# Edge stage of a graph layer on one core: VectorE's comparison moved, attribute product in bf16 parts, six waits dropped

## Chip, cores and metric

One Trainium2 chip, one of its cores. The time of a run is the device time of the whole program on that core, in microseconds (us). Engines: TensorE (PE; its weight loads are shown apart as PEld), VectorE (DVE), ScalarE (ACT), GpSimd (POOL) and SyncE (SP), which only issues transfers here. Lower is better.

## What is computed

One layer of a graph network over 50,000 nodes (x is 50000x128, float32) and 50,000 edges (src, dst, 16 attributes each), then a normalization. Edges come sorted by dst. The reference, cut to what matters:

```
edge_input = concat([x[row], x[col], edge_attr], axis=-1)   # row = src, col = dst
h = silu(edge_input @ eW1 + eb1)
m_ij = silu(h @ eW2 + eb2)
agg = segment_sum(m_ij, row, num_segments=50000)
update = silu(concat([x, agg]) @ nW1 + nb1) @ nW2 + nb2
out = layernorm(x + (x + update))
```

## The kernel before

The edges are cut into 98 groups (GROUP = 512 edges, four tiles of 128). Everything is written by hand, one instruction stream per engine, with semaphores between them; a wait on an engine holds all that stands behind it on that engine.

**Plan.** From the indices VectorE and TensorE work out for each edge a row of a table in HBM, in which edges of one source bucket sit together. Meanwhile ScalarE's queue fills that table with zeros and GpSimd gathers the x rows of the first 28 groups' sources.

**Edge loop**, group g on each engine:

- TensorE: the first layer's product for group g in three terms into p_h, attributes (L719), sources (L721), destinations (L723); then turn_dst(g+1) (L677, destinations by a one-hot `pick`), half of a self product for a node block (self_mm, L700), turn_src(g+1) (transposes, L664), q_mm(g-1) (L708, the message times w_agg), look_up(g+1) (L688), the other self half, and the second layer (L733).
- ScalarE: hT (L809), copy_xd (L792), two copies of the self product (L803), mT (L815).
- VectorE: copy_xs(g+1) out of PSUM (L1001), copy_q(g-1) out of PSUM (L1044, L1046), find_pos(g+1) (L1032 to L1038), compare_edges(g+2) (L1011 to L1023), which makes `pick`, `is_coarseT` and each edge's place in its tile.
- GpSimd: four indirect stores of group g's q rows into the table (L556), each followed by none or more indirect gathers of x rows for a group far ahead (L508). Its store of group g waits for copy_q(g).
- SyncE: loads edge rows, windows of x, attributes and node blocks, two to four groups ahead, and stores the self products.

The attributes lie in HBM transposed, 16 rows by all edges; SyncE loads 16x512 float32 a group (load_attr) into one of three buffers, after the product that used the buffer.

**Node stage.** After the last store SyncE reads the table block by block, and all engines sum per node, apply the two node layers and normalize. The change does not touch it.

Waits are given ahead of an instruction: one can ride on the instruction, each further one is an instruction of its own on the engine's queue.

Of the kernel before, what the change touches and what calls it, by code (L numbers as in the profile page):

```python
# [59 lines left out]
def gnn_kernel(nc, E, x, x_wide, xT, src_all, src_idx, dst_idx, dst_g, attrT, w1s, w1d, w1a, eb1, w2, eb2, nw1a, nb1, nw1b, nw2, nb2,  # L60
               out):
    N = x.shape[0]
    DE = attrT.shape[0]
# [23 lines left out]
    u0_dram = nc.dram_tensor("u0_dram", (STORED, P, BLOCK), F32, kind="Internal").ap()  # L87
    q_dram = nc.dram_tensor("q_dram", (P, D), F32, kind="Internal").ap()

    with ExitStack() as ctx:  # L90
# [15 lines left out]
        w_attr = sb("w_attr", [DE, D])  # L106
# [25 lines left out]
        attr = [sb(f"attr{s}", [DE, GROUP]) for s in range(ATTR)]  # L132
# [8 lines left out]
        with ExitStack() as plan:  # L141
# [21 lines left out]
            worst, worst_all, fits = tmp("worst", [P, 1]), tmp("worst_all", [1, 1]), tmp("fits", [1, 1])  # L163
            b_high, b_mid = tmp("b_high", [P, D], BF16), tmp("b_mid", [P, D], BF16)
# [58 lines left out]
        s_scattered = [sem(f"s_scattered{s}") for s in range(Q)]  # L223
        s_src_turned, s_dst_turned, s_pick, s_xsT, s_xdT = (
# [150 lines left out]
        def _(sp):  # L375
# [3 lines left out]
            for dst_sb, src_dram in ((w_src, w1s), (w_dst, w1d), (w_attr, w1a), (w_e2, w2), (w_agg, nw1b), (w_self, nw1a),  # L379
                                     (w_out, nw2)):  # L380
                sp.dma_start(dst_sb[:], src_dram).then_inc(s_weights, 16)
            for dst_sb, src_dram in ((b_e1, eb1), (b_e2, eb2), (b_n1, nb1)):
                sp.dma_start(dst_sb[:], src_dram.rearrange("(p a) -> p a", a=1)).then_inc(s_weights, 16)
# [15 lines left out]
            for g in range(ATTR):  # L399
                load_attr(g)  # L400
# [7 lines left out]
            sp.wait_ge(s_first_row, 16)  # L408
            sp.wait_ge(s_fits_i, 1)
# [41 lines left out]
            with sp.If_eq(sp.to_reg(fit), 1):  # L451
                load_windows(0)
                for g in range(-3, GROUPS):
                    load_edges(edges_dram[min(g + 3, GROUPS - 1)], g + 3)
                    load_windows(g + WINDOWS)
                    if g >= 0:
                        load_attr(g + 3)
                    serve_self(g)
            with sp.Else():
                pass_on_gathered(0)  # L460
                for g in range(-3, GROUPS):
# [3 lines left out]
                    if g >= 0:  # L465
                        load_attr(g + 3)

# [172 lines left out]
        def _(pe):  # L640
# [16 lines left out]
            def turn_src(g):  # L657
# [4 lines left out]
                wait(pe, s_xsT, g)  # L662
# [4 lines left out]
            def turn_dst(g):  # L667
# [5 lines left out]
                wait(pe, s_xdT, g)  # L673
# [37 lines left out]

            pe.wait_ge(s_before_tile, 1)
# [431 lines left out]
```

## Time and profile before

| | us |
|---|---|
| median of 3 runs | 1565.13 (1563.51 to 1565.4) |
| the profiled execution, its own time | 1560.06 |
| its span, first to last instruction | 1558.5 |
| PE busy | 1214.8 (78%) |
| POOL busy | 1046.3 (67%) |
| DVE busy | 753.9 (48%) |
| ACT busy | 464.9 (30%) |

TensorE's mean granted clock was 0.889 of full over the span. A busy time is the union of the recorded durations; of matmuls only the start is recorded, and the end is modelled. "remote" as the releaser of a wait means that the semaphore changed at a moment at which no instruction that updates it is recorded to end.

### The profile page before, as it was taken

To read this page: it belongs to the slowest core of one execution; us is meant where nothing else is said; L and a number is where in the kernel's file an instruction comes from. 1 tells how busy PE (TensorE), PEld (TensorE's weight loads), DVE (VectorE), ACT (ScalarE), POOL (GpSimd) and SP (SyncE) were. 2 spreads that over 40 slices of the span, in tenths; PEclk is the share of its full clock that TensorE was granted. 3 is DMA by queue.
4 is the path that set the end of the run, shared out by engine and by line. 5 is a ranking of instruction groups with operands and counts; after the bars stand their busy time and mean duration, and the time that the engine had idled before them with its cause. 6 is when DMAs were issued, how large, how long until landed. Compare 5 with 4: busy or idle time off the path is not lost.

```text
span 1558.5 us, 21182 instructions
## 1 busy us (share of the span) xinstructions
PE 1214.8 (78%) x6237; PEld 822.9 (53%) x6237; DVE 753.9 (48%) x2820; ACT 464.9 (30%) x846; POOL 1046.3 (67%) x1268
## 2 busy tenths in 40 slices
PE   3813677888898888979888877777777979999895
PEld 3812344454454444645554444444444579888884
DVE  8941244443344343433433433333333458888885
ACT  0000111222232222222222222222222247777774
POOL 8877565665666556656555666666666548899986
PEclk9996698898899888989888887988888979999998
DMA  9997334455565555655655554555454169999994
GB/s 339 413 411 257 94 106 117 140 166 164 158 200 174 160 165 162 191 171 163 185 164 167 158 154 150 164 164 155 155 153 135 53 228 411 410 410 410 407 407 168
DMA packets 183322, 333.48 MB, mean 214 GB/s; under 512 B 25648, under 2 KB 89696, under 8 KB 183205
## 3 DMA queue, kind: packets, MB, share of 16 engines
q1 hardware_dynamic: 136580, 211.68, 40.7%
q0 software_dynamic: 25024, 52.10, 11.3%
q10 hardware_dynamic: 21600, 68.32, 11.1%
q8 instruction: 52, 0.85, 0.2%
q14 instruction: 66, 0.53, 0.1%
HBM read 215.94 MB, written 116.06 MB: 213 GB/s over the span
## 4 chain that ended last, share of the span: by engine, by line
PE 45%; another core or an unknown queue 26%; DMA 8%; issue 7%; ACTq 7%; DVE 3%; ACT 2%; POOL 2%; POOLq 0%; SPq 0%; DVEq 0%
DMA ring<-table 8%; ACTq L782 7%; PE psum L677 6%; PE psum L751 6%; PE psum L721 6%; PE psum L719 5%; PE psum L700 5%; PE psum L733 5%; PE psum L723 5%; PE psum L708 3%; PE psum L766 3%; POOL table L556 1%; PE psum L664 1%; DVE work L1066 1%
## 5 line engine op out<-in xcount | busy, mean ns | idle before, releaser
L556 POOL DMA_INDIRECT table<-qs,pos x391 | 383.1, 980 | 334.8 <-DVE qs L1046 226.5
L508 POOL DMA_INDIRECT ring<-x_d,idx_src x391 | 408.2, 1044 | 119.1 <-issue 119.1
L1001 DVE COPY work<-psum 128x512 f32<-128x512 f32 x98 | 67.8, 692 | 554.4 <-remote 292.2
L677 PEld LDWEIGHTS psum<-work,windows 128*128 128x128 f32 x980 | 176.4, 200 | 147.5 <-issue 130.3
L677 PE MATMUL psum<-work,windows 128*128 128x256 f32 (+1 forms) x980 | 197.2, 350 | 59.0 <-issue 40.0
L700 PE MATMUL psum<-xT_in,w_self 128*128 128x320 f32 x314 | 129.5, 497 | 136.0 <-ACT u_out L803 101.0
L751 PE MATMUL psum<-work,ring 128*128 128x80 f32 x1250 | 157.3, 280 | 28.1 <-DVE work L1066 24.0
L751 PEld LDWEIGHTS psum<-work,ring 128*128 128x128 f32 x1250 | 148.9, 195 | 37.9 <-issue 21.1
L809 ACT ACTIVATE work<-psum,b_e 128x512 f32<-128x512 f32 x98 | 67.4, 687 | 322.0 <-PE psum L723 164.8
L721 PE MATMUL psum<-work,w_src 128*128 128x512 f32 x196 | 133.1, 766 | 36.7 <-DVE work L1001 20.8
L733 PE MATMUL psum<-work,w_e 128*128 128x512 f32 x196 | 122.1, 710 | 21.2 <-ACT work L809 21.2
L719 PE MATMUL psum<-attr,w_attr 16*128 16x512 f32 x196 | 128.3, 738 | 0.0
L700 PEld LDWEIGHTS psum<-xT_in,w_self 128*128 128x128 f32 x314 | 51.6, 207 | 141.6 <-issue 141.6
L1046 DVE COPY qs<-psum 128x512 f32<-128x512 f32 x98 | 67.5, 689 | 108.5 <-remote 88.8
L723 PE MATMUL psum<-work,w_dst 128*128 128x512 f32 x196 | 119.4, 696 | 0.0
L803 ACT COPY u_out<-psum 128x320 f32<-128x320 f32 x129 | 54.9, 425 | 202.9 <-remote 131.5
L1018 DVE SCALAR_TENSOR_TENSOR same<-edge_rows,bucket,earlier 128x128 f16<-128x128 f16 x392 | 114.0, 343 | 0.0
L792 ACT COPY work<-psum 128x512 f32<-128x512 f32 x98 | 57.4, 586 | 176.1 <-issue 86.0
L708 PE MATMUL psum<-w_agg,work 128*128 128x128 f32 x784 | 105.2, 277 | 3.5 <-ACT work L815 3.5
L815 ACT ACTIVATE work<-psum,b_e 128x512 f32<-128x512 f32 x98 | 67.5, 689 | 132.2 <-remote 74.7
L1011 DVE TENSOR_SCALAR work<-edge_rows,row_f 128x512 f32<-128x512 f16 x196 | 96.9, 536 | 19.4 <-DMA edge_rows<-edges_dram 19.2
L766 PE MATMUL psum<-w_out,work 128*128 128x128 f32 (+1 forms) x782 | 105.4, 282 | 0.0
(123 smaller groups left out, 1624.4 us busy)
## 6 DMA issues: line engine op xcount, KB each, us to landing
ring<-table SPq DMA_DIRECT2D x79, 528.0 KB, 11.1
table<-empty ACTq DMA_DIRECT2D x9, 4224.0 KB
edge_rows<-edges_dram SPq DMA_DIRECT2D x98, 384.0 KB
windows<-x_wide_d SPq DMA_DIRECT2D x98, 320.0 KB
xT_in<-xT_d SPq DMA_DIRECT2D x78, 320.0 KB
out<-windows ACTq DMA_DIRECT2D x78, 320.0 KB, 6.2
u_dram<-u_out SPq DMA_DIRECT2D x64, 320.0 KB
own_x<-x_d SPq DMA_DIRECT2D x48, 320.0 KB, 8.2
```

The lines of the kernel that those rows point to most:

```text
L508: pool.indirect_dma_start(rows, None, x[:, :], bass.IndirectOffsetOnAxis(ap=idx[:, g * TILES + t:g * TILES + t + 1], axis=0)).then_inc(don ...
L556: pool.indirect_dma_start(table[:, :], bass.IndirectOffsetOnAxis(ap=pos[:, g * TILES + t:g * TILES + t + 1], axis=0), q[g % Q][:, t, :], None,
L677: last = nc.tensor.matmul(p_dst[:, tiles], window[g % WINDOWS][:, j, :], pick[g % 2][:, places], start=j == 1, stop=j == 4, skip_group_che ...
L700: nc.tensor.matmul(p_self[:, 0:cols.stop - cols.start], w_self[:], xT_in[i % SELF][:, cols], start=True, stop=True).then_inc(s_self_mm, 1)
L708: last = nc.tensor.matmul(p_q[g % 2][:, t * D:(t + 1) * D], mT[g % 2][:, t * P:(t + 1) * P], w_agg[:], start=True, stop=True)
L719: nc.tensor.matmul(p_h, w_attr[:], attr[g % ATTR][:], start=True, stop=False)
L721: nc.tensor.matmul(p_h, w_src[:], xsT[g % 2], start=False, stop=False)
L723: nc.tensor.matmul(p_h, w_dst[:], xdT[g % 2], start=False, stop=True).then_inc(s_h_mm, 1)
L733: nc.tensor.matmul(p_m, w_e2[:], hT[g % 2], start=True, stop=True).then_inc(s_m_mm, 1)
L751: last = nc.tensor.matmul(u_bucket(b, k), slots_in[b % SLOTS_IN][:, k, 0:D], owner[b % 3][:, k, :].rearrange("s (r p) -> s r p", r=NODE_ROWS),
L766: last = nc.tensor.matmul(psum[2 + b % 2][0:p, j * D:(j + 1) * D], uT[b % 2][:, j * p:(j + 1) * p], w_out[:], start=False, stop=True, skip ...
L1018: last = V.scalar_tensor_tensor(out=same[:, t, :], in0=buckets[:, t * P:(t + 1) * P], scalar=bucket[:, c:c + 1], in1=earlier[:], op0=ALU.i ...
```

## The change

Three edits.

1. VectorE's loop: compare_edges(g+2) stands right behind copy_xs(g+1), ahead of copy_q(g-1) and find_pos(g+1).
2. The attribute term: each float32 is split into three bf16 parts. The host lays the attributes out by batches of 8 groups (128 rows by 512). For each batch VectorE makes the three parts (split_attr, four instructions), SyncE stores them twice to an HBM scratch (store_attr), and load_attr reads a 96-row bf16 tile a group from it: the three parts, twice. Two bf16 products, one of 96 rows (attributes' parts against the high and the middle part of the weights) and one of 48 rows (against the low part), replace the float32 product of 16 rows. The weights' parts are made once, by eight VectorE instructions (s_w_attr).
3. Six waits a group that other waits imply are left out: four on TensorE (s_xsT before turn_src, s_xdT before turn_dst, s_hT before the attribute product, s_mT before the second layer) and two on VectorE (s_dst_turned and s_look_mm in compare_edges).

The diff, without declarations and the host's reshaping:

```diff
             def load_attr(g):
                 if g >= GROUPS:
                     return
+                k, r = divmod(g, BATCH)
+                wait(sp, s_attr_out, 32 * (k + 1))
                 wait(sp, s_h_mm, g - ATTR + 1)
-                sp.dma_start(attr[g % ATTR][:], attrT[:, g * GROUP:(g + 1) * GROUP]).then_inc(s_attr[g % ATTR], 16)
+                rows = attr_dram[k, :, :, r * DE:(r + 1) * DE, :].rearrange("j i f e -> (j i) f e")
+                sp.dma_start(attr[g % ATTR][:], rows).then_inc(s_attr[g % ATTR], 16)
+
+            def store_attr(k):
+                sp.wait_ge(s_attr_split, 4 * (k + 1))
+                for j in range(2):
+                    sp.dma_start(attr_dram[k, j].rearrange("i p e -> p i e"), attr_parts[:]).then_inc(s_attr_out, 16)
+
+            def serve_attr(g):
+                k = g // BATCH + 1
+                if g < 0 or k >= BATCHES:
+                    return
+                if g % BATCH == 0:
+                    sp.wait_ge(s_attr_split, 4 * k)
+                    sp.dma_start(attr_left[:], attr_batches[k]).then_inc(s_attr_in, 16)
+                if g % BATCH == 4:
+                    store_attr(k)
...
-            for g in range(ATTR):
-                load_attr(g)
...
             sp.wait_ge(s_first_row, 16)
+            store_attr(0)
+            for g in range(ATTR):
+                load_attr(g)
             sp.wait_ge(s_fits_i, 1)
...
                     if g >= 0:
                         load_attr(g + 3)
+                    serve_attr(g)
                     serve_self(g)
...
                 wait(pe, s_gathered[pair(g)], pair_gathered(g))
-                wait(pe, s_xsT, g)
...
                 wait(pe, s_pick, g + 1)
-                wait(pe, s_xdT, g)
...
                 wait(pe, s_attr[g % ATTR], 16 * (g // ATTR + 1))
-                wait(pe, s_hT, g)
-                nc.tensor.matmul(p_h, w_attr[:], attr[g % ATTR][:], start=True, stop=False)
+                nc.tensor.matmul(p_h, w_attr_hm[:], attr[g % ATTR][:], start=True, stop=False)
+                nc.tensor.matmul(p_h, w_attr_l[0:PARTS, :], attr[g % ATTR][0:PARTS, :], start=False, stop=False)
...
                 wait(pe, s_hT, g + 1)
-                wait(pe, s_mT, g)
...
+            def split_attr(k):
+
+                wait(dve, s_attr_in, 16 * (k + 1))
+                wait(dve, s_attr_out, 32 * k)
+                V.tensor_copy(attr_parts[:, 0, :], attr_left[:]).then_inc(s_attr_split, 1)
+                dve.wait_ge(s_attr_split, 4 * k + 1)
+                V.tensor_tensor(attr_left[:], attr_left[:], attr_parts[:, 0, :], ALU.subtract).then_inc(s_attr_split, 1)
+                dve.wait_ge(s_attr_split, 4 * k + 2)
+                V.tensor_copy(attr_parts[:, 1, :], attr_left[:]).then_inc(s_attr_split, 1)
+                dve.wait_ge(s_attr_split, 4 * k + 3)
+                V.tensor_tensor(attr_parts[:, 2, :], attr_left[:], attr_parts[:, 1, :], ALU.subtract).then_inc(s_attr_split, 1)
...
                 wait(dve, s_edges[g % ROWS_IN], 16 * (g // ROWS_IN + 1))
-                wait(dve, s_dst_turned, g - 1)
...
                 last.then_inc(s_pick, 1)
-                wait(dve, s_look_mm, g - 1)
...
                 copy_xs(g + 1)
+                compare_edges(g + 2)
                 if g > 0:
                     copy_q(g - 1)
                 find_pos(g + 1)
-                compare_edges(g + 2)
+                if g % BATCH == 1 and g // BATCH + 1 < BATCHES:
+                    split_attr(g // BATCH + 1)
```

VectorE in the middle of the edge loop before, from copy_xs of one group to copy_xs of the next (work<-psum is xsT, qs is q):

```order
L1001 COPY work<-psum 128x512
L1044 COPY qs<-local 128x4
L1046 COPY qs<-psum 128x4x128
L1032 TENSOR_TENSOR hit<-psum,is_fine 128x20
L1035 TENSOR_REDUCE look<-hit 128x4
L1038 SCALAR_TENSOR_TENSOR pos<-look,base_row 128x4
L1011 TENSOR_SCALAR work<-edge_rows,row_f 128x4x128 x2
L1015 TENSOR_SCALAR is_coarseT<-edge_rows,row_f 128x512
L1018 SCALAR_TENSOR_TENSOR same,in_tile<-edge_rows,bucket,earlier 128x128 x4
L1023 SCALAR_TENSOR_TENSOR base_row<-in_tile,base_row 128x4
```

And the same stretch of the changed program (line numbers are those of the changed file):

```order
L1055 COPY work<-psum 128x512
L1064 TENSOR_SCALAR work<-edge_rows,row_f 128x4x128 x2
L1067 TENSOR_SCALAR is_coarseT<-edge_rows,row_f 128x512
L1070 SCALAR_TENSOR_TENSOR same,in_tile<-edge_rows,bucket,earlier 128x128 x4
L1075 SCALAR_TENSOR_TENSOR base_row<-in_tile,base_row 128x4
L1096 COPY qs<-local 128x4
L1098 COPY qs<-psum 128x4x128
L1084 TENSOR_TENSOR hit<-psum,is_fine 128x20
L1087 TENSOR_REDUCE look<-hit 128x4
L1090 SCALAR_TENSOR_TENSOR pos<-look,base_row 128x4
```

The copy of q and find_pos moved behind the eight instructions of the comparison. TensorE in the middle of the edge loop before, one group, with the semaphores that each row waits for:

```order
L719 MATMUL psum<-attr,w_attr 128x512 [waits s_hT,s_attr2]
L721 MATMUL psum<-work,w_src 128x512 [waits s_xsT]
L723 MATMUL psum<-work,w_dst 128x512 [waits s_xdT]
L677 MATMUL psum<-work,windows 128x256 [waits s_xdT,s_pick,s_window2]
...
L664 MATMUL psum<-ident,ring 128x128 [waits s_xsT,s_gathered2]
...
L708 MATMUL psum<-w_agg,work 128x128 [waits s_q,s_mT]
...
L733 MATMUL psum<-work,w_e 128x512 [waits s_mT,s_hT]
```

And of the changed program:

```order
L748 MATMUL psum<-attr,w_attr_hm 128x512 [waits s_attr0]
L749 MATMUL psum<-attr,w_attr_l 128x512
L751 MATMUL psum<-work,w_src 128x512 [waits s_xsT]
L753 MATMUL psum<-work,w_dst 128x512 [waits s_xdT]
L706 MATMUL psum<-work,windows 128x256 [waits s_pick,s_window2]
...
L694 MATMUL psum<-ident,ring 128x128 [waits s_gathered4]
...
L737 MATMUL psum<-w_agg,work 128x128 [waits s_q,s_mT]
...
L762 MATMUL psum<-work,w_e 128x512 [waits s_hT]
```

One attribute product became two, and four waits are gone. SyncE ahead of the loop in the changed program, where before the three attribute loads stood ahead of the store of first_dram:

```order
L433 DMA first_row<-first_dram 1x98 [waits s_plan_out]
L409 DMA attr_dram<-attr_parts 128x3x512 [waits s_attr_split,s_first_row]
L409 DMA attr_dram<-attr_parts 128x3x512
L404 DMA attr<-attr_dram 96x1x512 [waits s_attr_out] x3
L439 TENSOR_LOAD fits_i [waits s_fits_i]
```

The stores of batch 0 and the wait for them to land now stand between the plan and the first window's load.

## Rows read from the trace of the kernel before

**Rows 1.** Windows by stage: stretch, its length, then busy time of each engine, clock, DMA share, GB/s.

```profile
0.00:107.20 107.20, 51.80 (x413) 47.95 (x413) 89.66 (x128) 0.00 (x0) 86.74 (x78) 1.00 1.01 386
...
176.50:1208.00 1031.50, 836.95 (x3413) 491.35 (x3413) 399.28 (x1656) 239.20 (x432) 636.10 (x645) 0.88 0.53 159
...
1249.00:1558.50 309.50, 268.12 (x2189) 249.31 (x2189) 241.30 (x940) 209.33 (x391) 252.32 (x473) 0.95 0.92 358
```

**Rows 2.** Waits: who waited for whom, us in total, times, longest.

```profile
DVE work L1001 <- remote: 292.2, 32, 22.6
POOL table L556 <- DVE qs L1046: 226.5, 75, 5.2
```

**Rows 3.** Timeline, POOL (start, us, what): last early gather, first issues of runs, one last issue.

```profile
167.71 0.94 POOL L508 DMA_INDIRECT ring<-x_d,idx_src  x1 [0.30 <-issue]
...
700.52 0.97 POOL L556 DMA_INDIRECT table<-qs,pos  x1 [3.84 <-DVE qs L1046]
...
713.62 1.00 POOL L556 DMA_INDIRECT table<-qs,pos  x1 [4.39 <-DVE qs L1046]
...
724.53 0.98 POOL L556 DMA_INDIRECT table<-qs,pos  x1 [2.22 <-DVE qs L1046]
...
740.31 0.98 POOL L508 DMA_INDIRECT ring<-x_d,idx_src  x1 [0.30 <-issue]
...
745.26 1.00 POOL L556 DMA_INDIRECT table<-qs,pos  x1 [3.97 <-DVE qs L1046]
```

**Rows 4.** Timeline, PE: attribute and source products of three groups.

```profile
702.88 2.07 PE L719 MATMUL psum<-attr,w_attr 16*128 16x512 f32 x2
...
713.66 1.12 PE L719 MATMUL psum<-attr,w_attr 16*128 16x512 f32 x2
714.71 1.12 PE L721 MATMUL psum<-work,w_src 128*128 128x512 f32 x2
...
721.83 1.12 PE L719 MATMUL psum<-attr,w_attr 16*128 16x512 f32 x2
```

**Rows 5.** Timeline of all engines, 728 to 748, rows chosen.

```profile
728.62 1.06 PE L708 MATMUL psum<-w_agg,work 128*128 128x128 f32 x8
...
731.61 0.69 DVE L1046 COPY qs<-psum 128x512 f32<-128x512 f32 x1 [2.02 <-remote]
...
733.04 0.18 DVE L1032 TENSOR_TENSOR hit<-psum,is_fine 128x20 f32<-128x20 f32 x1 [0.73 <-remote]
733.22 1.02 PE L723 MATMUL psum<-work,w_dst 128*128 128x512 f32 x2
...
735.87 0.69 ACT L815 ACTIVATE work<-psum,b_e 128x512 f32<-128x512 f32 x1 [1.71 <-remote]
...
736.88 0.60 PE L664 MATMUL psum<-ident,ring 128*128 128x128 f32 x4
...
740.18 0.69 ACT L809 ACTIVATE work<-psum,b_e 128x512 f32<-128x512 f32 x1 [3.62 <-remote]
...
743.15 0.69 DVE L1001 COPY work<-psum 128x512 f32<-128x512 f32 x1 [7.16 <-remote]
...
747.15 2.07 PE L719 MATMUL psum<-attr,w_attr 16*128 16x512 f32 x2
```

**Rows 6.** Groups by line and form: the bf16 products of 512 columns in the node stage.

```profile
L762 PE MATMUL psum<-b_parts,ones_bf 128*128 128x512 bf16 x78 | 29.8, 382 | 0.0
```

**Rows 7.** Timeline, DVE: first and last instruction of one compare_edges.

```profile
700.65 1.06 DVE L1011 TENSOR_SCALAR work<-edge_rows,row_f 128x512 f32<-128x512 f16 x2
...
703.09 0.23 DVE L1023 SCALAR_TENSOR_TENSOR base_row<-in_tile,base_row 128x4 f32<-128x4 f32 x1
```

**Rows 8.** Groups by line, DVE: the nearest rows to split_attr's instructions.

```profile
L902 DVE TENSOR_TENSOR dst_rel<-dst_i,tile_i 98x512 f32<-98x512 int32 x1 | 0.6, 644 | 0.0
...
L912 DVE CAST edges_b<-coarse 98x512 f16<-98x512 f32 x1 | 0.4, 422 | 0.0
```

**Rows 9.** Timeline, DVE: the first compare_edges of the loop.

```profile
102.36 0.88 DVE L1011 TENSOR_SCALAR work<-edge_rows,row_f 128x512 f32<-128x512 f16 x2 [10.09 <-DMA edge_rows<-edges_dram]
```

More of the change, by code:

```diff
@@ L87, in gnn_kernel @@
     u0_dram = nc.dram_tensor("u0_dram", (STORED, P, BLOCK), F32, kind="Internal").ap()
+    attr_dram = nc.dram_tensor("attr_dram", (BATCHES, 2, 3, P, GROUP), BF16, kind="Internal").ap()
     q_dram = nc.dram_tensor("q_dram", (P, D), F32, kind="Internal").ap()
@@ L131, in gnn_kernel @@
         xsT, xdT, hT, mT = ([work[:, (4 + 2 * k + s) * GROUP:(5 + 2 * k + s) * GROUP] for s in range(2)] for k in range(4))
-        attr = [sb(f"attr{s}", [DE, GROUP]) for s in range(ATTR)]
+        attr = [sb(f"attr{s}", [TWICE, GROUP], BF16) for s in range(ATTR)]
+        attr_left, attr_parts = sb("attr_left", [P, GROUP]), sb("attr_parts", [P, 3, GROUP], BF16)
         is_coarseT = [sb(f"is_coarseT{s}", [P, GROUP], F16) for s in range(2)]
@@ L223, in gnn_kernel @@
         s_scattered = [sem(f"s_scattered{s}") for s in range(Q)]
+        s_attr_in, s_attr_split, s_attr_out, s_w_attr = (sem(n) for n in ("s_attr_in", "s_attr_split", "s_attr_out", "s_w_attr"))
         s_src_turned, s_dst_turned, s_pick, s_xsT, s_xdT = (
@@ L466, in _ @@
                         load_attr(g + 3)
+                    serve_attr(g)
             sp.wait_ge(s_src_turned, GROUPS)
@@ L710, in q_mm @@
                 last.then_inc(s_q_mm, 1)
+            pe.wait_ge(s_w_attr, 8)
             pe.wait_ge(s_before_tile, 1)
@@ L991, in _ @@
                                    ).then_inc(s_b_parts, 1)
+            V.tensor_copy(w_high[:], w_attr[:]).then_inc(s_w_attr, 1)
+            V.tensor_scalar(is_first[:], row_f[0:TWICE, 0:1], PARTS - 0.5, None, ALU.is_lt).then_inc(s_w_attr, 1)
+            V.tensor_scalar(is_second[:], row_f[0:TWICE, 0:1], PARTS - 0.5, None, ALU.is_gt).then_inc(s_w_attr, 1)
+            dve.wait_ge(s_w_attr, 3)
+            V.tensor_tensor(w_attr[:], w_attr[:], w_high[:], ALU.subtract).then_inc(s_w_attr, 1)
+            V.tensor_scalar(w_sum[:], w_high[:], is_first[:, 0:1], None, ALU.mult).then_inc(s_w_attr, 1)
+            dve.wait_ge(s_w_attr, 5)
+            V.tensor_copy(w_mid[:], w_attr[:]).then_inc(s_w_attr, 1)
+            dve.wait_ge(s_w_attr, 6)
+            V.tensor_tensor(w_attr_l[:], w_attr[:], w_mid[:], ALU.subtract).then_inc(s_w_attr, 1)
+            V.scalar_tensor_tensor(out=w_attr_hm[:], in0=w_mid[:], scalar=is_second[:, 0:1], in1=w_sum[:], op0=ALU.mult,
+                                   op1=ALU.add).then_inc(s_w_attr, 1)
             dve.wait_ge(s_ids, 1)
@@ L1118, in by_block, with by_batch @@
         return rows
+    def by_batch(attr):
+        batch, de = P // attr.shape[1], attr.shape[1]
+        groups = -(-padded_edges(E) // (GROUP * batch)) * batch
+        rows = np.zeros((groups * GROUP, de), attr.dtype)
+        rows[:E] = attr
+        return rows.reshape(groups // batch, batch, GROUP, de).transpose(0, 1, 3, 2).reshape(groups // batch, P, GROUP)
     no_node = ((-(-N // BLOCK) * BLOCK) + BUCKET * np.arange(pads)).astype(src.dtype)
```

18 lines of the change are left out of this document (13 added, 5 removed).

## The prediction

> **What bounds the kernel now.** I read the windows by stage first [rows 1]. The edge loop proper, groups 2 to 93, fills 176.5 to 1208: 1031.5 us for 92 groups, 11.2 us each. TensorE is busy in 837 of them and GpSimd in 636, so no engine is full. The node stage (309.5 us) and the table fill ahead of the loop (DMA share 1.01 until 107.2) don't contain an edited line that matters, so the question is what an average group of 11.2 us waits for.
>
> A group in which TensorE waits for nothing takes 8.17 us: from the start of one attribute product to the next, 713.66 to 721.83, at full clock [rows 4]. The missing 3 us a group come in lumps. GpSimd's issues tell the rhythm: it restarts after a pause at 700.52, 713.62, 724.53 and 745.26 [rows 3]. Between the first and the last lie 44.7 us and 27 issues of 1.28 us (0.98 and 0.30 between them), that is four groups' q: 34.6 us of issues and 10.1 us of pauses. Each pause ends with copy_q, and over the run GpSimd waited for it 75 times, 226.5 us [rows 2].
>
> Next, what makes q late. In the last third of that cycle TensorE's records run ahead of what the other engines see [rows 5]. The products of q end at 729.68 by the record (728.62 + 1.06), and VectorE is let go at 731.61; the first layer ends at 734.24, and ScalarE starts hT at 740.18, 5.9 us later; the transposes end at 737.48, and VectorE copies xs at 743.15, 5.7 us later. All three consumers had been idle. So TensorE's signals arrive late. They do so only inside long GpSimd runs: this run began at 724.53 and its last issue ended at 741.29 [rows 3], and by 743.15 everything was released at once. Signals in the first microseconds of a run, or while GpSimd rests, are on time; q's at 731.61, 7.1 us into this run, is the first late one. VectorE's wait for xs with releaser "remote", 292.2 us in 32 waits [rows 2], is this. During the late stretch signals are spaced: q's at 731.61 and the look-up's at 733.04, 1.43 us apart, though the look-up is four products of five columns each and has two waits. That reads as 0.71 us for each wait that TensorE passes in such a stretch. Between mT's release at 735.87 and hT's at 740.18 lie four waits and three products, 4.3 us, which does not contradict it (2.97 us of products by the record, or six such steps).
>
> When TensorE then idles for its own chain through ScalarE it comes back at half clock (1.2 GHz instead of 2.4): the attribute product takes 2.0 us instead of 1.05 [rows 5, 4].
>
> So a cycle of four groups is: restart, one group at half clock, one or two at 8.17 us, and then a stretch paced by late signals that ends only when GpSimd has run dry. There are 92/4 = 23 cycles in the loop.
>
> **The change, part by part, in that cycle.**
>
> *Attribute product.* Removed: 1.05 us a group at full clock, 2.0 at half. Added: two bf16 products of 512 columns, of which the rows here have one kind, 0.38 us on the mean over both clocks [rows 6]; two make 0.76. A float32 product of 512 columns takes 1.05 from its start to the next one's [rows 4]; the mean of 0.38 mixes both clocks, and at full clock a bf16 one should lie below it, so I take 0.55 for the pair: minus 0.5 a group at full clock, minus 1.0 at half. Bounds: minus 0.3 (0.76) and minus 0.8. The Trainium skill, TensorE: Matmul & The Clock Gate, section Back-to-back issue gap, gives N/2.4 + 2.5 ns for a bf16 product, 0.43 us for the pair, whatever the number of rows; by it the term is minus 0.6, and the sum 3 us lower. It helps only where TensorE's work and not a late signal decides when q is ready: two of the four groups, one of them at half clock. Minus 1.5 a cycle, times 23: **minus 35** (bounds minus 15 and minus 50).
>
> *Waits on TensorE.* Nineteen a group become fifteen. At full speed a wait that is already satisfied costs nothing that a row shows. In the late stretch I price the four at 0.71 us each, 2.8 us. About one group a cycle passes all of them in that state: minus 2.8, times 23, **minus 64**. Bounds: 0, if the spacing comes from something else than the waits, and minus 128, if two groups a cycle profit. The two waits left out on VectorE belong to signals that its earlier wait for turn_src implies: nothing.
>
> *compare_edges ahead of copy_q.* It lasts 2.67 us (700.65 to 703.32) [rows 7]. Its place behind copy_xs costs nothing where q isn't there yet: then it fills a wait (731.61 was such a wait). Where xs and q are released together, as at 743.15, q is copied 2.67 us later, and GpSimd, which is dry, restarts 2.67 us later. What is queued behind it on VectorE is copy_q and find_pos; who waits is GpSimd (L556), and TensorE's look_up and q_mm only a group later. That is once a cycle for sure, plus 2.67 times 23: **plus 62**. Bounds: 0 (during that pause TensorE's signals are on time, so the time is used) and plus 124 (in the next group too, where xs and q again come within 1 us). I take the middle because the pause at 713.62 ends with a q that TensorE had only just finished.
>
> *split_attr.* Two casts of 0.42 and two subtractions of 0.64 [rows 8], 2.1 us, 12 times in the loop, after find_pos, where an unhindered group leaves VectorE 2 us idle. **Plus 8**, bounds 0 and 26. Its load (256 KB) and stores (768 KB) each eight groups, and 64 KB more a group for the tile, add some 190 KB to a group at a DMA share of 0.53 [rows 1]: hidden, and the bound is inside this range. Their waits on SyncE are a group or more old when they are reached; what stands behind them there is the next edge rows and window.
>
> *Ahead of the loop.* SyncE now waits for 768 KB to land before the first window, among the fill at a DMA share of 1.01. The nearest row: the first edge rows took VectorE's 10.1 us of waiting [rows 9]. The first window and edge rows come up to 15 us later. But GpSimd's early gathers run until 169 [rows 3] and the signals free up only then, so most of it lies beside them: **plus 5**, bounds 0 and 15. The eight instructions on the weights' parts and the first split_attr (some 4 us) lie in the same cover. Last four groups, TensorE-bound: **minus 2**.
>
> Sum: -35 - 64 + 62 + 8 + 5 - 2 = -26 us on the profiled execution's 1560.06, so 1534. The median of the runs is 5 us above that execution; I forecast 1539.
>
> **Rivals.**
>
> *GpSimd is held back more than TensorE gains (slower).* Place: the restart after each long run. Price: 2.67 us twice a cycle, plus 124, and the late signals are not paced by waits, so that term is 0: 1560 - 35 + 124 + 26 + 10 - 2 = 1683 in full; halfway 1600. It decides from the point where the compare term exceeds the two gains, 99 us, that is 4.3 us a cycle. For it: three of the four pauses of the cycle end with copy_q soon after copy_xs. Against: GpSimd's dry time is what frees TensorE's signals.
>
> *The late stretch collapses.* If TensorE passes a late group in 2.8 us less, GpSimd's run may be broken in time and the long stretch of four-group cycles shrinks for good: half of the 292 us of remote waits gone, less the compare term: about 1560 - 35 - 128 + 62 + 11 = 1470.
>
> *The terms cancel.* GpSimd's 8.6 us of issues a group and its pause of 2.5 us, in which the signals come free, stay the pace, whatever TensorE does: 1565. The row of pauses speaks for it, since two of the three end right after TensorE's signals are released.
>
> *The clock.* TensorE has less to do in a group and may be found idle more often. In the trace it fell to 1.2 GHz after each idle stretch in a late phase and not inside groups of 8.17 us. A group at half clock costs 10.8 instead of 8.17 us (702.88 to 713.66) [rows 4]. The Trainium skill, TensorE: Matmul & The Clock Gate, section The HAM clock gate, has it that activity releases the throttle and an idle engine is throttled; by that rule thinner groups could fall more often. By the rows one more such group a cycle is 2.6 times 23, plus 60: 1599. Little speaks for it, as the product that shrinks is 0.5 of 8.17 us.
>
> **Chances.** Forecast, between 0.5 and 4% faster: 0.47. Collapse of the late stretch: 0.15. GpSimd held back, slower: 0.23; clock, slower: 0.06. Cancelling: 0.09, of which within 0.2% (about what a measurement tells here): 0.06. That makes faster 0.64, same 0.06, slower 0.30. The likeliest case alone spans 1505 to 1557. For 8 in 10 the range takes in most of both rivals: 1475 to 1600.
>
> **What would show it.** In the changed profile: the attribute pair starting 0.5 to 0.6 us before the source product; a full-speed group of 7.6 us; compare_edges directly behind copy_xs; GpSimd's pause after a long run 6.5 us instead of 4; ScalarE's L809 released earlier in a late stretch; fewer and shorter "remote" waits on VectorE's copy of xs. The forecast is wrong if the spacing of late signals stays at 1.4 and 4.3 us with the waits gone, if the restarts of GpSimd move out by more than 4 us a cycle, or if the loop starts later than 180 us.

## The result and the profile after

The changed kernel takes 1603.09 us (median of 4 runs, 1597.18 to 1605.38) beside 1564.32 for the kernel before (4 runs). The ratio is 1.0255 (95% interval 1.0207 to 1.0303), so 2.55% slower, some 40 us. Here and below a ratio is worked out from the single runs, without one that lies over 1.5% above the fastest of its kernel, so it can differ by some tenths of a per cent from the quotient of the medians. The profiled execution took 1604.12 us, its span 1602.4, at a mean granted clock of 0.874 of full.

Starts of attribute products tell where the time went. First the kernel before (timeline of TensorE; group 93 and group 97), then the changed one (groups 2, 93 and 97):

```profile
1204.17 2.07 PE L719 MATMUL psum<-attr,w_attr 16*128 16x512 f32 x2
...
1235.37 1.12 PE L719 MATMUL psum<-attr,w_attr 16*128 16x512 f32 x2
```

```profile
181.05 0.38 PE L748 MATMUL psum<-attr,w_attr_hm 96*128 96x512 bf16 x1
...
1243.62 0.38 PE L748 MATMUL psum<-attr,w_attr_hm 96*128 96x512 bf16 x1
...
1277.92 0.38 PE L748 MATMUL psum<-attr,w_attr_hm 96*128 96x512 bf16 x1
```

Group 2 started at 176.5 before [rows 1], so the setup costs 4.6 us more. Groups 2 to 92 take 1062.6 us (1243.62 - 181.05) where they took 1027.7 (1204.17 - 176.5): 34.9 more. Groups 93 to 96 take 34.3 instead of 31.2, 3.1 more, and all that follows 324.5 instead of 323.1. Together 44, the difference of the spans. The loss is in the loop.

Windows of the changed kernel, columns as in [rows 1], the loop and the node stage:

```profile
181.00:1243.50 1062.50, 784.32 (x3409) 487.35 (x3408) 406.98 (x1697) 236.31 (x430) 631.20 (x636) 0.84 0.55 170
1291.00:1602.40 311.40, 272.10 (x2194) 252.38 (x2192) 241.07 (x940) 210.69 (x393) 254.64 (x474) 0.95 0.91 356
```

TensorE has some 50 us less to do in the loop (784 for 837), GpSimd about the same (631 for 636), and it still takes longer. The two waits of [rows 2], in the changed kernel:

```profile
DVE work L1055 <- remote: 456.9, 40, 30.7
POOL table L587 <- DVE qs L1098: 256.0, 56, 6.6
```

GpSimd waits for copy_q 56 times instead of 75, but 4.6 us each instead of 3.0. The total is 29.5 us larger. One such pause is this (timeline of all engines, rows chosen; the row at 732.69 is GpSimd's last issue before it, the last row its first issue after it):

```profile
723.89 0.38 PE L748 MATMUL psum<-attr,w_attr_hm 96*128 96x512 bf16 x1
...
724.20 0.39 PE L749 MATMUL psum<-attr,w_attr_l 48*128 48x512 bf16 x1
...
724.52 1.12 PE L751 MATMUL psum<-work,w_src 128*128 128x512 f32 x2
...
728.78 0.60 PE L694 MATMUL psum<-ident,ring 128*128 128x128 f32 x4
...
729.73 0.69 ACT L844 ACTIVATE work<-psum,b_e 128x512 f32<-128x512 f32 x1 [1.71 <-remote]
...
730.47 1.16 PE L737 MATMUL psum<-w_agg,work 128*128 128x128 f32 x8 [1.09 <-ACT work L844]
...
732.69 0.98 POOL L587 DMA_INDIRECT table<-qs,pos  x1 [0.30 <-issue]
735.51 0.59 ACT L821 COPY work<-psum 128x512 f32<-128x512 f32 x1 [2.21 <-remote]
735.62 0.69 DVE L1055 COPY work<-psum 128x512 f32<-128x512 f32 x1 [7.30 <-remote]
...
736.23 0.87 DVE L1064 TENSOR_SCALAR work<-edge_rows,row_f 128x512 f32<-128x512 f16 x2
736.57 1.41 PE L729 MATMUL psum<-xT_in,w_self 128*128 128x320 f32 x2 [4.54 <-ACT u_out L832]
...
738.63 0.68 DVE L1098 COPY qs<-psum 128x512 f32<-128x512 f32 x1
...
739.48 0.63 PE L748 MATMUL psum<-attr,w_attr_hm 96*128 96x512 bf16 x1
...
739.59 0.97 POOL L587 DMA_INDIRECT table<-qs,pos  x1 [5.92 <-DVE qs L1098]
```

Read it from the top. The attribute pair starts 0.63 us ahead of the source product (1.05 before). The transposes for xs end at 729.4 and the products of q at 731.6 by the record. GpSimd, in a long run, issues its last transfer at 732.69 and is dry at 733.67. TensorE's signals come free 1.9 us after that, at 735.5 to 735.6. VectorE then copies xs, makes the comparison from 736.23 on, and copies q at 738.63, 3.0 us after xs. GpSimd restarts at 739.59, after 5.92 us. Before, such a pause was 3.97 us (741.29 to 745.26) [rows 3]. There copy_q followed copy_xs directly; here the comparison's 2.4 us lie between them, and GpSimd's restart comes some 2 us later.

An undisturbed group is as forecast: 7.65 us from 747.53 to 755.18 (before 8.17 [rows 4]).

```profile
747.53 0.38 PE L748 MATMUL psum<-attr,w_attr_hm 96*128 96x512 bf16 x1
...
755.18 0.38 PE L748 MATMUL psum<-attr,w_attr_hm 96*128 96x512 bf16 x1
```

### The profile page after: what moved, and what is told of

Its sections match the earlier page's. It is cut to its first block, busy times and chain, and to the rows that moved or that the text cites. A ratio compares the mean times of both kernels' runs of the same rounds, so it can differ in the third digit from the quotient of the medians.

```text
span 1602.4 us, 21002 instructions
## 1 busy us (share of the span) xinstructions
PE 1163.2 (73%) x6237; PEld 820.1 (51%) x6237; DVE 767.0 (48%) x2880; ACT 463.0 (29%) x846; POOL 1051.5 (66%) x1268
## 4 chain that ended last, share of the span: by engine, by line
another core or an unknown queue 35%; PE 31%; issue 10%; DVE 9%; POOL 6%; DMA 5%; ACT 2%; SPq 1%; POOLq 0%; ACTq 0%
PE psum L706 5%; PE psum L751 4%; PE psum L729 4%; PE psum L780 4%; PE psum L762 4%; PE psum L753 3%; DMA ring<-table 3%; POOL windows L662 3%; PE psum L795 2%; DVE work L952 2%; DMA edge_rows<-edges_dram 1%; PE psum L737 1%; POOL table L587 1%; DVE work L1055 1%
## 5 line engine op out<-in xcount | busy, mean ns | idle before, releaser
L587 POOL DMA_INDIRECT table<-qs,pos x391 | 387.4, 991 | 365.2 <-DVE qs L1098 256.0
L1055 DVE COPY work<-psum 128x512 f32<-128x512 f32 x98 | 67.8, 692 | 638.0 <-remote 456.9
L729 PE MATMUL psum<-xT_in,w_self 128*128 128x320 f32 x314 | 135.3, 517 | 211.1 <-ACT u_out L832 125.5
L706 PE MATMUL psum<-work,windows 128*128 128x256 f32 (+1 forms) x980 | 192.7, 345 | 26.1 <-issue 26.1
L751 PE MATMUL psum<-work,w_src 128*128 128x512 f32 x196 | 129.2, 745 | 70.3 <-DVE work L1055 69.9
L762 PE MATMUL psum<-work,w_e 128*128 128x512 f32 x196 | 131.2, 758 | 17.4 <-ACT work L838 17.4
L737 PE MATMUL psum<-w_agg,work 128*128 128x128 f32 x784 | 107.3, 281 | 16.9 <-ACT work L844 13.6
L753 PE MATMUL psum<-work,w_dst 128*128 128x512 f32 x196 | 112.2, 657 | 0.0
L737 PEld LDWEIGHTS psum<-w_agg,work 128*128 128x128 f32 x784 | 97.5, 195 | 21.3 <-ACT work L844 16.9
L1064 DVE TENSOR_SCALAR work<-edge_rows,row_f 128x512 f32<-128x512 f16 x196 | 87.9, 490 | 34.6 <-DMA edge_rows<-edges_dram 26.1
L795 PEld LDWEIGHTS psum<-w_out,work 128*128 128x128 f32 (+1 forms) x782 | 95.6, 195 | 9.5 <-issue 0.6
```

Source lines behind the costliest of these rows:

```text
L587: pool.indirect_dma_start(table[:, :], bass.IndirectOffsetOnAxis(ap=pos[:, g * TILES + t:g * TILES + t + 1], axis=0), q[g % Q][:, t, :], None,
L706: last = nc.tensor.matmul(p_dst[:, tiles], window[g % WINDOWS][:, j, :], pick[g % 2][:, places], start=j == 1, stop=j == 4, skip_group_che ...
L729: nc.tensor.matmul(p_self[:, 0:cols.stop - cols.start], w_self[:], xT_in[i % SELF][:, cols], start=True, stop=True).then_inc(s_self_mm, 1)
L737: last = nc.tensor.matmul(p_q[g % 2][:, t * D:(t + 1) * D], mT[g % 2][:, t * P:(t + 1) * P], w_agg[:], start=True, stop=True)
L751: nc.tensor.matmul(p_h, w_src[:], xsT[g % 2], start=False, stop=False)
L753: nc.tensor.matmul(p_h, w_dst[:], xdT[g % 2], start=False, stop=True).then_inc(s_h_mm, 1)
```

## The experiments

**The theory and its rivals.** Theory A: GpSimd's issues in the loop are a fixed amount, its pauses are added to them, and each pause ends with copy_q; what stands ahead of copy_q after TensorE's signals come free is paid. Rival B: the bf16 attribute path costs the time. Rival C: TensorE, with fewer waits, runs into the late stretch more often. Rival D came with the first four runs: it depends on the chip. Rivals E to H are named in the expectations where they are tested.

**The chips differ.** The kernel before was measured anew beside each set of runs, on six chips. It took 1562.72, 1570.51, 1571.87 and (two visits to one chip) 1578.88 and 1561.33 us on four of them, but 1350.54 (31 runs) and 1353.12 us (31 runs) on the other two. I call the last two the on-time chips. Most edits were measured on a chip of either kind; the bf16 path alone was measured on an on-time chip only, and the last two kernels below on the other kind only. Only one chip was visited twice, so chip and visit are not told apart on the others; on that one the kernel before differed by 1.1% between the visits. All ratios are to the kernel before on the same chip and visit.

*Each part alone, on an on-time chip.* Four kernels: before with the new place of compare_edges alone; before without the six waits alone; before with the bf16 path alone; the changed kernel with compare_edges back in its old place.

> The kernel before with one edit alone: compare_edges stands behind copy_xs and ahead of copy_q. Theory A (the moved comparison holds GpSimd back; the 2.67 us come at most restarts): 1600 us, the whole loss of the change or more, and GpSimd's run/pause cycle is the one of the changed kernel (runs of about 20 us, VectorE's wait for xs with releaser remote above 400 us). Rival B (the bf16 attribute path costs it, through its DMAs and the later start of the loop): within 5 us of before, about 1565. Rival C (TensorE without the four waits gets into the late-signal phase more often): also about 1565.

> The kernel before with only the six implied waits left out. Theory A: no change or a gain of up to 64 us, as my prediction had it; I now expect less, 1555 to 1565, because the records of the changed kernel still show long late stretches. Rival C (fewer waits let TensorE issue earlier into a long GpSimd run, so more of its signals are late): 1580 to 1600.

> The kernel before with only the bf16 attribute path (parts made by VectorE, stored and loaded by SyncE, two bf16 products). Theory A: 0.5 us less TensorE work a group against a later start of the loop by 5 us and split_attr: 1550 (1540 to 1565). Rival B (the path costs what the change lost): 1585 to 1605.

> The changed kernel with compare_edges put back behind find_pos, all else as changed. Theory A: 1545 (1525 to 1560), below before. Rivals B and C: 1595 to 1605, as the changed kernel.

Measured: 1352.74 (ratio 1.0021, 1.0011 to 1.0031), 1350.47 (1.0003, 0.9993 to 1.0012), 1351.03 (1.0004, 0.9993 to 1.0015) and 1349.46 us (0.9997, 0.9987 to 1.0006). The expectations took a kernel before of 1565 us; here it was 215 us faster, so its times can't be set beside theirs. Waits in the run without the six waits (its line 997 is copy_xs, 556 GpSimd's store, 508 its gather):

```profile
DVE work L997 <- PE psum L663: 370.8, 90, 13.6
...
POOL table L556 <- issue: 117.6, 386, 0.3
POOL ring L508 <- issue: 116.6, 383, 0.3
```

There is no wait for a "remote" signal on xs, and GpSimd waits for nobody: 0.3 us between one issue and the next, 769 times. GpSimd's issues stand end to end from the first gather to the last store of the loop, and none of the edits shows beyond 0.2%.

*The changed kernel as it is, on another chip.*

> The changed kernel as it is, beside the kernel before, to see in which regime this chip runs. In the four runs above both kernels took 1350 us and no TensorE signal was late (VectorE's wait for xs had TensorE's transposes as releaser, none was remote). Theory D (the 2.5% loss exists only where TensorE's signals arrive late during long GpSimd runs; else GpSimd's 782 issues of 1.3 us are the bound and every edit is hidden): if the kernel before takes 1350 us here, the changed one takes 1350 to 1356; if before takes 1565, the changed one takes 1600. Rival A (the order of the comparison costs time anywhere): 1375 or more beside 1350.

Measured: 1598.5 us (1595.55 to 1611.37, 6 runs) beside 1562.72, ratio 1.0257 (1.0208 to 1.0306). The loss is real, repeats, and was seen only where TensorE's signals come late. From here on the arguments rest on such chips alone.

*The order alone.* The kernel before with

```diff
                 copy_xs(g + 1)
+                compare_edges(g + 2)
                 if g > 0:
                     copy_q(g - 1)
                 find_pos(g + 1)
-                compare_edges(g + 2)
```

> The order alone again, in the hope of a chip on which before takes 1560 (the first four ran on one where both kernels take 1350 and no signal is late). Theory A: 1595 to 1605, ratio about 1.025, with longer remote waits on VectorE's copy of xs. Rival B or C: ratio 0.995 to 1.005.

Measured: 1638.05 us beside 1570.51, ratio 1.0387 (1.0336 to 1.0438), 61 us of 1565. I had expected 1.025; this one edit costs more than the whole change. Its waits:

```profile
DVE work L1001 <- remote: 461.9, 37, 18.0
POOL table L556 <- DVE qs L1046: 295.0, 61, 6.7
```

GpSimd's wait for copy_q grew by 68.5 us against [rows 2], from 3.0 to 4.8 us a time. GpSimd's busy time over the whole span is 1046.8 us here and 1046.3 in the kernel before: in these two executions the time is added in pauses alone.

*The waits alone.* The kernel before without the six waits:

> The six waits alone again, for the same reason. My prediction's term: minus 64 (ratio 0.96, 1500). Theory A now: within 10 us of before. Rival C: 1580 to 1600.

Measured: 1566.83 us beside 1570.51, ratio 0.9975 (0.9948 to 1.0001): 4 us, at most 8, where I had forecast 64. A late stretch of this run (line 1040 is copy_q, 1026 find_pos, 811 mT, 805 hT, 997 copy_xs):

```profile
600.76 0.69 DVE L1040 COPY qs<-psum 128x512 f32<-128x512 f32 x1 [2.10 <-remote]
602.21 0.18 DVE L1026 TENSOR_TENSOR hit<-psum,is_fine 128x20 f32<-128x20 f32 x1 [0.76 <-remote]
605.05 0.69 ACT L811 ACTIVATE work<-psum,b_e 128x512 f32<-128x512 f32 x1 [1.00 <-remote]
609.38 0.69 ACT L805 ACTIVATE work<-psum,b_e 128x512 f32<-128x512 f32 x1 [3.63 <-remote]
612.36 0.69 DVE L997 COPY work<-psum 128x512 f32<-128x512 f32 x1 [7.20 <-remote]
```

From q to look-up it is 1.45 us, from look-up to mT 2.84, from mT to hT 4.33. In the kernel before it was 1.43, 2.83 and 4.31 (731.61, 733.04, 735.87, 740.18) [rows 5]. Two of the four waits left out stood in these stretches, one between look-up and mT, one between mT and hT. The spacing did not move.

*More waits.* The kernel before with each of the four implied waits given three times, as here:

```diff
                 wait(pe, s_gathered[pair(g)], pair_gathered(g))
                 wait(pe, s_xsT, g)
+                wait(pe, s_xsT, g)
+                wait(pe, s_xsT, g)
```

> The kernel before with each of the four implied TensorE waits given three times, eight more satisfied waits a group. My prediction's price (0.71 us a wait in the late stretch, about one group a cycle): plus 128, 1690. Theory H (late signals are not paced by waits; leaving four out had changed the time by 4 us): within 10 us of before.

> Eight more satisfied waits a group on TensorE, again, for a chip on which before takes 1560. My prediction's price (0.71 us a wait in the late stretch, about one group a cycle): plus 128, 1690. Theory H (late signals are not paced by waits): within 15 us of before, and the late signals of q and of the look-up still 1.43 us apart.

On an on-time chip 1352.17 us (0.9997, 0.9987 to 1.0007). On one with late signals 1558.48 us (1543.87 to 1569.65) beside 1571.87, ratio 0.9891 (0.9848 to 0.9935): where 128 us more were due by my price, it took 1% less. The eight waits are only four instructions more a group on TensorE's queue (the page counts 21570 instructions for 21182 before), since two waits can share one there; not each further wait is an instruction of its own, as the description of the kernel before has it. Per instruction my price would still be some 65 us. Two late stretches of it (line 1054 is copy_q, 1040 find_pos, 823 mT, 817 hT):

```profile
680.03 0.69 DVE L1054 COPY qs<-psum 128x512 f32<-128x512 f32 x1 [3.64 <-remote]
...
681.47 0.98 POOL L556 DMA_INDIRECT table<-qs,pos  x1 [1.40 <-DVE qs L1054]
681.48 0.18 DVE L1040 TENSOR_TENSOR hit<-psum,is_fine 128x20 f32<-128x20 f32 x1 [0.75 <-remote]
682.24 0.69 ACT L823 ACTIVATE work<-psum,b_e 128x512 f32<-128x512 f32 x1 [0.30 <-remote]
683.72 0.69 ACT L817 ACTIVATE work<-psum,b_e 128x512 f32<-128x512 f32 x1 [0.79 <-remote]
...
762.42 0.69 DVE L1054 COPY qs<-psum 128x512 f32<-128x512 f32 x1 [2.12 <-remote]
763.88 0.18 DVE L1040 TENSOR_TENSOR hit<-psum,is_fine 128x20 f32<-128x20 f32 x1 [0.77 <-remote]
...
768.16 0.69 ACT L823 ACTIVATE work<-psum,b_e 128x512 f32<-128x512 f32 x1 [2.42 <-remote]
...
771.16 0.98 POOL L508 DMA_INDIRECT ring<-x_d,idx_src  x1 [0.30 <-issue]
...
773.18 0.69 ACT L817 ACTIVATE work<-psum,b_e 128x512 f32<-128x512 f32 x1 [4.33 <-remote]
```

With the same six waits between them, mT and hT are released 1.48 us apart in the one stretch and 5.02 us in the other; between look-up and mT stand six waits too (two of them ahead of the self product), and it is 0.76 us and 4.28 us. So the count of waits does not set the spacing. The two stretches differ in what GpSimd did: in the first it had run dry at 680.07 and began anew at 681.47, in the second it issued on, with no gap over 0.71 us, until 772.14. Why this kernel was 1% faster stays open.

*The waits and the bf16 path, old order.* The changed kernel with compare_edges back behind find_pos:

> The changed kernel with compare_edges put back behind find_pos, again. Theory A: 1525 to 1560, below before. Rivals B and C: 1590 to 1605. Against the run with the waits alone it gives the price of the bf16 attribute path: minus 35 by my prediction, plus 20 or more by rival B.

Measured: 1561.76 us beside 1570.51, ratio 0.9934 (0.991 to 0.9958), 10 us. Less the waits' 4 the bf16 path gives 6 us, but the two intervals (up to 0.9958, from 0.9948) overlap, so its own share is not clear of noise. Putting the order on top takes it to 1.0255 on other chips: a factor of 1.032, 50 us.

*Half of the comparison.* Only its first three instructions (pick twice, is_coarseT; 1.2 of 2.67 us) ahead of copy_q, as pick_edges, which compare_edges then leaves out:

```diff
                 copy_xs(g + 1)
+                pick_edges(g + 2)
                 if g > 0:
                     copy_q(g - 1)
                 find_pos(g + 1)
                 compare_edges(g + 2)
```

> The kernel before with only the first three instructions of the comparison (pick and is_coarseT, 1.2 us of the 2.67) ahead of copy_q, the other five left behind find_pos. Theory A (so many us a pause): a bit under half of the full move's 61 to 67 us, 1587 to 1600, ratio 1.014 to 1.022. Rival G (the move tips the cycle into another pattern whatever its length): the full 1.039.

> The half move (pick and is_coarseT ahead of copy_q, 1.2 of 2.67 us) again, for a chip on which before takes 1560. Theory A (so many us a pause of GpSimd): 1587 to 1600, ratio 1.014 to 1.022. Rival G (the move tips the cycle into another pattern whatever its length): 1.035 to 1.04. Rival F (it costs only through find_pos, which comes as much later): as A here, told apart by the run with the comparison between copy_q and find_pos.

On an on-time chip 1355.52 us (1.0023, 1.0012 to 1.0033). With late signals 1616.22 us beside 1578.88, ratio 1.0238 (1.0192 to 1.0285), 37 us. That is 61% of the full move's loss for 45% of its time, a little above theory A's range and below rival G's 1.035: more like a dose than a switch, but not a straight line either.

*Ahead of find_pos only.* copy_xs, copy_q, compare_edges, find_pos:

```diff
                     copy_q(g - 1)
+                compare_edges(g + 2)
                 find_pos(g + 1)
-                compare_edges(g + 2)
```

> The kernel before with compare_edges moved ahead of find_pos, but not of copy_q. Theory A (only the delay of q counts): ratio 0.995 to 1.005. Rival F (what costs is that find_pos, and with it the rows' places and TensorE's next look-up, comes later): 1.02 to 1.04, like the full move.

> compare_edges ahead of find_pos but not of copy_q, again, for a chip on which before takes 1560. Theory A (only the delay of q counts): ratio 0.995 to 1.005. Rival F (find_pos, and with it the rows' places and TensorE's next look-up, comes later, and that costs): 1.02 to 1.04.

1353.52 us on an on-time chip (1.0006, 0.9996 to 1.0016), and with late signals 1563.88 beside 1561.33, ratio 1.0029 (1.0001 to 1.0056). find_pos and the next look-up come 2.67 us later here as in the full move, and it costs 0.3%, not 3.9%. So what costs is the comparison's place ahead of copy_q, and with it the delay of q.

*q copied first.*

```diff
-                copy_xs(g + 1)
                 if g > 0:
                     copy_q(g - 1)
+                copy_xs(g + 1)
```

> The kernel before with copy_q(g-1) moved one place up, ahead of copy_xs(g+1). Theory A (each pause of GpSimd ends with copy_q, so what stands ahead of it after the signals' release is paid once a pause, and there are some 72 pauses of 3.1 us in the loop): the pause loses the 0.69 us of copy_xs, 1520 to 1550 beside 1565. Rival E (TensorE, which then gets its xs 0.6 us and a wait for q later, paces the cycle): 1565 to 1610. If this chip is one on which before takes 1350, no difference by any theory.

> copy_q(g-1) ahead of copy_xs(g+1) again, for such a chip. Theory A: the pause loses 0.69 us, 1520 to 1550. Rival E (TensorE then gets xs later and its own chain paces the cycle): 1565 to 1610.

1353.85 us on an on-time chip (1.0005, 0.9995 to 1.0014). With late signals 1565.13 beside 1578.88, ratio 0.9914 (0.9888 to 0.9939): a gain as theory A says, but 14 us where I had expected 15 to 45. The time misses the 1520 to 1550 that I had given, and rival E's slower kernel did not come. GpSimd's wait for q is 207.1 us in 72, 19 less than in [rows 2].

*The best of both.* The changed kernel with compare_edges back behind find_pos and copy_q first; and the same with copy_q cut in two:

```diff
-                V.tensor_copy(q[g % Q][:, :, 0:D], p_q[g % 2]...).then_inc(s_q, 1)
+                V.tensor_copy(q[g % Q][:, 0:1, 0:D], from_psum[:, 0:1, :]).then_inc(s_q, 1)
+                V.tensor_copy(q[g % Q][:, 1:TILES, 0:D], from_psum[:, 1:TILES, :]).then_inc(s_q, 1)
...
-                wait(pool, s_q, 2 * (g + 1))
+                wait(pool, s_q, 3 * g + 2)
                 wait(pool, s_pos, g + 1)
                 for t in range(tiles_of(g)):
+                    if t == 1:
+                        wait(pool, s_q, 3 * (g + 1))
```

> The changed kernel with compare_edges back behind find_pos, copy_q(g-1) ahead of copy_xs(g+1), and copy_q's 512 columns cut in two: the first 128 with a signal of their own, on which GpSimd starts the first of its four stores. Theory A (the pause is what can be shortened): the gains of q first (0.9%) and of waits and bf16 (0.7%) add up, and the cut takes up to 0.5 us off some 70 pauses: 1515 to 1550, ratio 0.965 to 0.985. Rival E (the rest of the pause is set by when TensorE's signals come free, and shorter copies only shift it): 0.985 to 0.995. On a chip on which before takes 1350: 1345 to 1355.

> The run with the cut copy of q (ratio 0.966), without the cut: the changed kernel with compare_edges behind find_pos and copy_q ahead of copy_xs. If the cut gave most of the gain: 0.98 to 0.99. If q first, bf16 and waits gain more together than alone (0.9%, 0.4%, 0.25%): 0.965 to 0.975.

Without the cut 1530.54 us beside 1561.33, ratio 0.9809 (0.9765 to 0.9854). With it 1521.66 beside 1571.87, ratio **0.9659** (0.9587 to 0.9732): 3.4% below the kernel before, and both kernels are beaten. The uncut kernel with the gains of q first (0.9%), bf16 and waits (0.7%) added up would stand at 0.985, inside its interval. Against q first alone (0.9914, the same chip on another visit) bf16 and waits give 1.1%, some 17 us, more than the 10 us in the old order; whether that surplus is real no run here settles. GpSimd's waits for copy_q, first in the uncut kernel, then in the cut one (line 1101 is the first piece of the copy, 1102 the second) with two rows of its timeline:

```profile
POOL table L587 <- DVE qs L1098: 182.5, 73, 3.9
```

```profile
POOL table L589 <- DVE qs L1101: 136.8, 65, 3.4
...
POOL table L589 <- DVE qs L1102: 49.2, 19, 3.7
```

```profile
708.75 0.29 DVE L1101 COPY qs<-psum 128x128 f32<-128x128 f32 x1 [6.86 <-PE psum L739]
...
709.32 0.97 POOL L589 DMA_INDIRECT table<-qs,pos  x1 [1.75 <-DVE qs L1101]
```

This pause is 1.75 us, of which VectorE's part is the 0.29 us copy and the way from it to GpSimd; VectorE was let go 1.18 us after GpSimd's last issue had ended at 707.57. But over the run the cut does not shorten GpSimd's waits for copy_q: 136.8 and 49.2 make 186.0 us in 84, where the uncut kernel has 182.5 in 73, and GpSimd's idle time is 473 us of the span in one as 474 in the other (1520.6 less 1047.6 busy, 1532.5 less 1058.8). The two ratios are 1.5% apart, the times themselves 9 us, and they come from two chips. So what the cut gave, and by what, is not shown.

| kernel (chips with late signals) | ratio | GpSimd's wait for copy_q: us, times |
|---|---|---|
| before | 1 | 226.5, 75 |
| comparison ahead of q | 1.0387 | 295.0, 61 |
| half of it ahead of q | 1.0238 | 276.9, 68 |
| changed kernel | 1.0255 | 256.0, 56 |
| comparison behind q, ahead of find_pos | 1.0029 | 227.8, 73 |
| six waits out | 0.9975 | 220.0, 74 |
| waits out, bf16 | 0.9934 | 222.4, 72 |
| q first | 0.9914 | 207.1, 72 |
| eight more waits | 0.9891 | 217.6, 78 |
| q first, waits out, bf16 | 0.9809 | 182.5, 73 |
| the same, copy of q cut | 0.9659 | 186.0, 84 (both pieces) |

The third column is from one execution each. On the whole the time rises with it; four neighbouring pairs are out of order: changed kernel and half move, bf16 and six waits out, q first and eight more waits, and the last two rows.

## Why the prediction was wrong

I forecast 1539 us, a gain of 1.7%; the kernel takes 1603, 3 us beyond the range, on the side to which I gave 0.30.

**The step that failed** is "In the late stretch I price the four at 0.71 us each": a term of minus 64 that is minus 4 (at most minus 8). The spacing that I read as waits does not come from them: it stayed at 1.45, 2.84 and 4.33 us with the waits gone, the outcome that I had named as the refutation. Two facts of the rows had been stretched into a rate: 1.43 us with two waits, and 4.3 us with four waits. Of the second I could say only that it "does not contradict it". A term priced on one spacing was the largest of the sum. Its lower bound, 0, was near the right value. With 0 there my own sum is -35 + 62 + 8 + 5 - 2 = plus 38: 1598 on the profiled execution and 1603 on the median. That this sum hits is luck in part: the attribute path with what it costs stands in it at minus 24 and measured minus 6, the order stands at plus 62 and measured 50 on top of the rest, and the waits, here at 0, measured minus 4.

**compare_edges ahead of copy_q**, plus 62: measured 61 alone, 50 on top of the rest. The mechanism is as given: q and xs are released together, q is copied 2.4 us later, GpSimd restarts later. What I did not see is that the count of pauses changes too: 61 of 4.8 us for 75 of 3.0. So once a cycle, 23 times 2.67, is not how the cost comes about, and the agreement of 62 with 61 is luck in part as well. By the half move and by q first, a microsecond ahead of copy_q is worth 20 to 31 us over the loop, against my 23.

**The attribute path** was to give 35 and cost 8 and 5, minus 24 with the last groups: measured minus 6, with the caution above. In the trace every piece is there: the pair in 0.63 us where I had taken 0.55 (the 0.38 us of [rows 6] is no mean over both clocks, as I read it, but what one such product is recorded with at a granted clock of 1.00, at 723.89, while the next starts 0.31 us after it), the full-speed group at 7.65 us, split_attr's four instructions in 2.3 us (725.98 to 728.31), the first comparison 20 us later but group 2 only 4.6 us later. The mistake, as I read it, is in "two of the four groups": a group that runs faster between two pauses doesn't move a pause, since TensorE's signals come free only behind GpSimd's run. That is argued; no run tests it apart. The Trainium skill, TensorE: Matmul & The Clock Gate, section Back-to-back issue gap, gives N/2.4 + 2.5 ns for a single product at the full clock, an estimate of 0.43 us for the pair. The trace has 0.63, so the figure is too low for these two products of 96 and 48 rows.

**Two more mistakes in the prediction.** It has one late stretch in a cycle of four groups, from 731.61 on. But the run from 713.62 had a late one too: q's products ended at 720.31, GpSimd ran dry at 722.31 (2.22 us ahead of 724.53 [rows 3]), and the copy began only at

```profile
723.56 0.69 DVE L1046 COPY qs<-psum 128x512 f32<-128x512 f32 x1 [3.31 <-remote]
```

And the sum of the rival "The late stretch collapses" takes 128 for half of 292, which is 146.

**The rivals.** "GpSimd is held back more than TensorE gains" is what happened, with its time (halfway 1600) and half of its mechanism: the late signals are not paced by waits. Its other half, the price twice a cycle, did not come. "The terms cancel" had the right reason for TensorE's side: GpSimd's issues and pauses set the pace, and less work on TensorE gave 6 us. It lacked that the order makes the pauses longer. The late stretch did not collapse: the wait for xs with releaser remote rose from 292.2 to 456.9 us. The clock fell, 0.88 to 0.84 in the loop: after 4.54 us of idling TensorE starts at 736.57 at a granted clock of 0.50, and the attribute product at 739.48 takes 0.63 us and not 0.38. The Trainium skill, TensorE: Matmul & The Clock Gate, section The HAM clock gate, has the idle engine throttled and activity releasing the throttle. The trace agrees. I take the lower clock for a result of the longer pauses; no run here prices it apart.

## What to carry to other kernels

Find the engine whose busy time is nearly the same in every version (GpSimd, 1039 to 1059 us in all profiles of the slower kind of chip), and look at what ends its pauses: here an instruction's place behind the release of a wait was worth 3.9% one way (2.67 us ahead of the copy) and 0.9% the other (0.69 us less), while half a microsecond less work a group on the busiest engine gave 0.4%, not clear of noise. In this kernel a fill for an idle engine belongs behind the instruction that restarts the next engine, not ahead of it, even if it usually fits into the wait. And a price per wait read from one spacing is a guess until an experiment has changed the number of waits; until then the sum should be made with the price at its lowest bound as well, and where that changes the sign of the answer, the forecast should say so.

## What the hardware showed

The same program took 1350 to 1353 us on two chips and 1561 to 1579 us on four. Up to 107.2 us the traces agree: there GpSimd is busy for 86.74 us on both kinds, and the DMA share is 1.01. They part behind it: from 107.2 to 150 the kernel without the six waits has TensorE busy for 19.25 us on a chip of the one kind and for 29.99 on an on-time chip. Issues back to back are not enough for it, since GpSimd's gathers had followed each other without a pause from 4.1 us on. In the loop TensorE's signals are held back on four chips while GpSimd issues (the first late one in [rows 5] 7.1 us into the run) and in the pauses shown they come free 1.2 to 1.9 us after its last issue ends (722.31 to 723.56 above, 733.67 to 735.51 in the changed kernel, 741.29 to 743.15 in [rows 3, 5]). VectorE's and ScalarE's signals are on time inside such runs: in the changed kernel mT ended at 730.42 and TensorE's L737 started at 730.47, 13 us into a run, and here, 17 us into another, the copy ended at 1208.42:

```profile
1207.73 0.69 DVE L1055 COPY work<-psum 128x512 f32<-128x512 f32 x1 [11.13 <-remote]
...
1208.47 2.07 PE L751 MATMUL psum<-work,w_src 128*128 128x512 f32 x2 [0.92 <-DVE work L1055]
```

Between one release and the next lie 0.76, 1.43 to 1.48, 2.84, 4.28 to 4.33 and 5.02 us, about 1, 2, 4, 6 and 7 times 0.71. The steps are regular in the few rows shown, but how many of them lie between two signals did not follow the number of waits. What on the chip holds the signals back, and why only on some chips, no run here shows. Runs of GpSimd broken up on purpose, or without its gathers, would be the next thing to try; that was not done.
